# The last group of a two-layer decoder: its tail beside the shared expert, the router's choice inside the expert blocks, inner rows of the final feed-forward in the wait for a gather, and bulk loads issued earlier

## What is computed

```python
for e in range(E):
    m = topi == e
    sel = m.any(axis=-1)
    wmean = (topw * m).sum() / jnp.maximum(m.sum(), 1)
    y = _mlp(xf, expert_gate_w[e], expert_up_w[e], expert_down_w[e])
    out = out + jnp.where(sel[:, None], y * wmean, 0)
out = out + _mlp(x, shared_gate_w, shared_up_w, shared_down_w)
```

## Time and profile before

| | us |
|---|---|
| median of 3 runs | 2366.88 (2365.27 to 2369.79) |
| profiled execution | 2361.88 |
| its span, first to last instruction | 2360.1 |
| PE / DVE / ACT / POOL busy | 1914.0 / 1671.1 / 1110.2 / 846.1 |
| mean granted TensorE clock | 0.908 of full speed |

### The profile page before, as it was taken

The page is one execution under the profiler, slowest core; times in us unless marked ns, Lnnn a source line. Parts: engine busy times, 40 slices in busy tenths (PEclk is TensorE's granted clock), DMA queues, the critical chain, the costliest instruction groups (busy, mean ns, idle before and its releaser), DMA issues.

```text
span 2360.1 us, 39753 instructions
## 1 busy us (share of the span) xinstructions
PE 1914.0 (81%) x14136; PEld 1359.2 (58%) x14136; DVE 1671.1 (71%) x4073; ACT 1110.2 (47%) x3152; POOL 846.1 (36%) x775
## 2 busy tenths in 40 slices
PE   2786688878897898788898789789887889775698
PEld 1455356745685467645685457645774568563355
DVE  8895795679947794769756994789567975713355
ACT  3463266435653466436642566246543565332243
POOL 0552363316512462327421661336332652111000
PEclk7997799979997999889997999799988999787799
DMA  3000010402040012201040103001130204070000
GB/s 133 11 1 10 12 61 6 128 10 72 1 122 12 24 58 60 74 19 63 6 126 12 38 36 116 18 23 59 30 104 10 72 1 129 5 256 19 10 14 23
DMA packets 72748, 117.09 MB, mean 50 GB/s; under 512 B 7823, under 2 KB 46871, under 8 KB 72039
## 3 DMA queue, kind: packets, MB, share of 16 engines
q1 hardware_dynamic: 67014, 101.42, 13.3%
q0 software_dynamic: 5536, 13.12, 1.9%
HBM read 95.18 MB, written 18.81 MB: 48 GB/s over the span
## 4 chain that ended last, share of the span: by engine, by line
DVE 38%; PE 35%; issue 12%; POOL 6%; ACT 6%; DMA 3%; SPq 1%; DVEq 0%; POOLq 0%; ACTq 0%
PE bank L1392 32%; DVE work L513 11%; DVE bank L522 5%; DVE work L531 3%; DVE work L511 3%; ACT work L984 3%; POOL hid L1298 2%; DVE max L821 2%; PE bank L1396 2%; POOL work L1278 1%; ACT act_row L984 1%; DMA y_sorted<-y_quad 1%; POOL work L1273 1%; DVE acc L733 1%; DMA w_ring<-in_w_routed 1%
## 5 line engine op out<-in xcount | busy, mean ns | idle before, releaser
L1392 PEld LDWEIGHTS bank<-work 128*128 128x128 f32 (+2 forms) x5152 | 388.4, 200 | 164.2 <-issue 160.6
L1392 PE MATMUL bank<-work 128*128 128x128 f32 (+2 forms) x5152 | 419.6, 308 | 50.2 <-DMA work<-in_wo 25.4
L984 ACT ACTIVATE work<-bank 128x512 f32<-128x512 f32 (+1 forms) x560 | 246.9, 519 | 275.9 <-PE bank L1392 244.7
L513 DVE TENSOR_TENSOR work<-bank,table_space 64x512 f32<-64x512 f32 x512 | 352.2, 688 | 6.8
L1266 POOL TENSOR_TENSOR work<-work 128x512 f32<-128x512 f32 x128 | 163.4, 1277 | 332.7 <-DVE work L513 231.3
L984 ACT ACTIVATE work<-work 128x512 f32<-128x512 f32 (+1 forms) x338 | 196.6, 618 | 140.6 <-DVE work L601 81.4
L984 ACT ACTIVATE work<-work,negmax 128x128 f32<-128x128 f32 x512 | 199.2, 390 | 100.2 <-DVE negmax L533 100.2
L1273 POOL TENSOR_TENSOR work<-sb_ident,nrm 128x512 f32<-128x512 f32 x128 | 133.2, 1041 | 275.0 <-ACT nrm L984 275.0
L1392 PE MATMUL bank<-work,table_space 128*128 128x512 f32 x256 | 140.4, 630 | 89.9 <-DVE negmax L533 59.4
L984 ACT ACTIVATE hid<-bank,w_ring 128x128 f32<-128x128 f32 x480 | 136.4, 370 | 138.3 <-PE bank L1392 138.2
L511 DVE TENSOR_TENSOR work<-bank,table_space 128x512 f32<-128x512 f32 x256 | 173.8, 679 | 30.2 <-POOL work L1278 18.3
(11 more groups left out here) (293 smaller groups left out, 3327.2 us busy)
## 6 DMA issues: line engine op xcount, KB each, us to landing
w_ring<-in_w_routed SPq DMA_DIRECT2D x120, 514.0 KB, 4.8
x_quad<-x_sorted SPq DMA_DIRECT2D x24, 256.0 KB, 2.9
y_sorted<-y_quad SPq DMA_DIRECT2D x24, 256.0 KB, 4.4
x_T<-in_x_T POOLq DMA_DIRECT2D x9, 256.0 KB, 3.0
x_row<-in_x_row POOLq DMA_DIRECT2D x9, 256.0 KB, 4.1
ctx_T<-in_ctx_T SPq DMA_DIRECT2D x8, 256.0 KB, 2.7
work<-in_ctx_row SPq DMA_DIRECT2D x8, 256.0 KB, 3.1
out<-act_row SPq DMA_DIRECT2D x8, 256.0 KB, 2.3
```

Source lines behind the costliest of these rows:

```text
L513: last = v.tensor_tensor(rows(wk[i + 1][o]), rows(src[p]), sinT[o, s].unsqueeze(1).broadcast_to([DH0, GB, N]), ALU.mult)
L984: return nc.scalar.activation(o, i, f, **k)
L1392: return nc.tensor.matmul(o, l, r, start=start, stop=stop, skip_group_check=True)
```

## The change

Six edits, all in the last group and phase 2.

1. **Tail beside the shared expert.** `last_experts` replaces `heads_and_experts(G - 1, ...)` on PE, ACT and DVE. On PE the tail of group 6 is interleaved with the shared expert; on DVE its two layernorms use `inverse_root`; POOL issues four of the eight scatters before its part of the tail.
2. **SP order.** The bulk loads go ahead of `first_blocks(G - 1)`, for groups 0 to 5; group 6's and 7's activations are copied from SBUF by `keep_tail`; the five first weight loads go ahead of the wait for the scatter.
3. **Choice in two halves.** `choose` runs in five steps, for groups 0 to 6 between the blocks of the last group, for group 7 where the whole choice was.
4. **Seven `block_up`s early.** All five of group 0 and two of group 1 are issued right behind the last block, and PE, DVE and ACT do them before `experts_norm`. Their results lie in the weight ring.
5. **`experts_norm`** takes its root from DVE.
6. **Phase 2** starts with what is left of group 1, before the means are known; the down products of groups 0 and 1 follow in two runs. The choice is transposed straight from `sel1`, without a copy on POOL.

```diff
@@ SP
+            def keep_tail(g):
+                sp.wait_ge(t_T_sb, g * LNS + LNS)
+                sp.dma_start(x5T_all[:, g], seq_T[:]).then_inc(stored, 16)
+                sp.dma_start(x5_all[:, g], act_row[0][:].rearrange("p b d -> p (b d)")).then_inc(stored, 16)
             def first_blocks(g):
+                if g == G - 1:
+                    sp.wait_ge(owners_in, g + 1)
+                    for j in range(RING):
+                        load_weights(j)
                 sp.wait_ge(scattered, g * (TOPK * GB * 16) + TOPK * GB * 16)
...
             g = G - 1
-            store_tail(g, -1)
-            first_blocks(g)
             sp.wait_ge(attn_out, G)
             for name in phase2:
                 sp.dma_start(late[name], a[name]).then_inc(in2, 16)
-            sp.wait_ge(stored, 32 * g + 16)
-            sp.dma_start(x5T_all[:, 0:g], ...); sp.dma_start(x5_all[:, 0:g], ...)
+            sp.wait_ge(stored, 32 * (g - 1) + 16)
+            sp.dma_start(x5T_all[:, 0:g - 1], ...); sp.dma_start(x5_all[:, 0:g - 1], ...)
+            first_blocks(g)
+            keep_tail(g - 1)
             blocks(g)
-            sp.wait_ge(t_T_sb, g * LNS + LNS)
...
+            keep_tail(g)
@@ DVE
+            def choose(step, lo, k):
+                n = k * GB
...
+                if step == 0:
+                    dve.wait_ge(rl_a, 2 if lo else 1)
+                    link(v.tensor_scalar(ex, ex, 1.0, None, ALU.add))
+                    link(v.reciprocal(pr, ex))
+                if step == 1:
+                    best(pr, oh1, m1)               # five instructions
+                    link(v.scalar_tensor_tensor(t, oh1, -4.0, pr, ALU.mult, ALU.add))
+                if step == 2:
+                    best(t, oh2, m2)
...
+            def last_experts(g):
+                for i in (1, 2):
+                    if i == 1:
+                        tail_out(g, -1)
+                    else:
+                        tail_mix(g, -1)
+                    dve.wait_ge(norm_t.stats, tally(g, -1, LNS, i + 1))
+                    inverse_root(norm_t)
+                    centre_of(norm_t, g, i, -1)
+                tail_logits(g, -1)
+                take_rows(0, g)
+                add_shared(g)
+                for i in range(BLOCKS):
+                    take_block(i, g)
+                    if i in (1, 5, 9):
+                        take_rows(i // GB + 1, g)
+                    if i in (3, 5, 7, 9, 11):
+                        choose((i - 3) // 2, 0, G - 1)
+                dve.wait_ge(in2, in2_all)
+                v.tensor_copy(sel2b[:], late["sel2"]).then_inc(sel_cast, 1)
+                for p in range(BLK):
+                    hidden1(p, 0)
+                for p in range(AHEAD):               # AHEAD = 2
+                    hidden1(p, 1)
@@ ACT
+            def last_experts(g):
+                norm_tail(g, 1, bank[2], act_row[1], -1, True)
+                gelus(0, g)
+                t_to_T(g, 1, bank[7], -1)
+                norm_tail(g, 2, bank[6], act_row[0], -1, True)
+                gelus(1, g)
+                t_to_T(g, 2, bank[2], -1)
+                router_exps(0, G - 1)
+                for j in range(2, UNITS):
+                    gelus(j, g)
+                choices1(0)
+                for p in range(PAIRS):
+                    silu1(p, 0)
...
@@ POOL
-            tail(G - 1, -1)
             pool.wait_ge(slots_in, G)
-            for i in range(TOPK * GB):
+            for i in range(GB):
                 scatter(G - 1, i)
+            tail(G - 1, -1)
+            for i in range(GB, TOPK * GB):
+                scatter(G - 1, i)
@@ PE
+            def last_experts(g):
+                tail_out(g, -1)
...
+                experts_up(0, g, 0, False)
+                tail_mix(g, -1)
+                experts_up(1, g, 0, False)
+                tail_T(g, -1)
+                experts_down(0, g, 0, False)
+                tail_logits(g, -1)
+                experts_down(1, g, 0, False)
+                rows_T(0, g, 0, False)
+                experts_up(2, g, 0, False)
+                for j in range(3, UNITS + 1):
...
+                pe.wait_ge(in2, in2_all)
+                choices_of(0)
+                for p in range(BLK):
+                    if p == PAIRS:
+                        choices_of(1)
+                    block_up(p, 0)
+                for p in range(AHEAD):
+                    block_up(p, 1)
+            last_experts(G - 1)
+            pe.wait_ge(h_done, BLK + AHEAD)
             project2(G - 1, False)
             attn1(G - 1, G, False)
...
+            for p in range(AHEAD, PAIRS):
+                block_up(p, 1)
+            choices_of(2)
+            pe.wait_ge(sums_done, 2)
...
+            block_up(PAIRS, 1)
+            pe.wait_ge(norm_f.out, 1)
...
+            block_up(0, 2)
+            for p in range(BLK):
+                block_down(p, 0)
+            block_up(1, 2)
+            for p in range(BLK):
+                block_down(p, 1)
```

More of the change, by code:

```diff
@@ L286, in first_blocks @@
                 load_rows(1)
-                for j in range(RING):
-                    load_weights(j)
+                if g < G - 1:
+                    for j in range(RING):
+                        load_weights(j)
             def blocks(g):
@@ L1848, in _, with choices_of @@
                 attn1(g, g + 2, True)
-            heads_and_experts(G - 1, 1, False, True, True)
+            def choices_of(k):
+                pe.wait_ge(sums_done, 1 if k < G - 1 else 2)
+                if k == 0:
+                    pe.wait_ge(y_out, G * BLOCKS)
+                else:
+                    pe.wait_ge(selT_sb, k)
+                for b in range(GB):
+                    last = nc.tensor.transpose(bank[6][0:8, b * N:b * N + N], sel1[:, k, b], ident[:])
+                last.then_inc(selT_ps, 1)
@@ new lines, in block_down @@
+            def block_down(p, g):
+                pe.wait_ge(h_done, g * BLK + p + 1)
+                if p == 0 and g == 0:
+                    pe.wait_ge(scaled, 1)
+                elif p == 0:
+                    pe.wait_ge(sum_read, g)
+                for b in range(GB):
+                    last = mm(rows(bank[7])[:, b], rows(hidden_tile(g, p))[:, b], late["w_d1"][:, p],
+                              start=p == 0 and b == 0, stop=p == BLK - 1)
+                if p == BLK - 1:
+                    last.then_inc(y4, 1)
@@ L1855, in _ @@
             tail_logits(G - 1, 0)
-            pe.wait_ge(sums_done, 1)
-            mm(bank[0][0:8, 0:1], router_sum[:, 0], ones_col)
-            mm(bank[0][0:8, 1:2], router_sum[:, 1], ones_col, start=False).then_inc(tot, 1)
-            pe.wait_ge(in2, in2_all)
+            for p in range(AHEAD, PAIRS):
+                block_up(p, 1)
+            choices_of(2)
+            pe.wait_ge(sums_done, 2)
+            for i in range(2):
+                for half in range(2):
+                    last = mm(bank[7][0:8, i:i + 1], router_sum[:, half, i], ones_col, start=i + half == 0)
@@ L1886, in block_down @@
-            def block_down(p, g, d):
-                pe.wait_ge(h_done, tally(g, d, BLK, p + 2))
-                if p == 0:
-                    pe.wait_ge(sum_read, tally(g, d, 1, 1))
-                for b in range(GB):
-                    last = mm(rows(bank[7])[:, b], rows(wk[2 + p])[:, b], late["w_d1"][:, p],
-                              start=p == 0 and b == 0, stop=p == BLK - 1)
-                if p == BLK - 1:
-                    last.then_inc(y4, 1)
-            def ffn1(g, d, before):
-                block_up(0, g, d)
-                if before:
-                    block_down(BLK - 1, g, d - 1)
-                for p in range(1, BLK):
-                    if p == PAIRS:
-                        transpose_choices(tally(g, d, 1, 2))
-                    block_up(p, g, d)
-                    block_down(p - 1, g, d)
@@ L1908, in _ @@
[L1908 to L1912 removed]
+            block_up(0, 2)
[4 more added lines that the diff above has]
+                block_down(p, 1)
+            block_up(2, 2)
+            block_down(0, 2)
+            block_down(1, 2)
+            block_up(3, 2)
+            block_down(2, 2)
@@ L1915, in layouts @@
+            choices_of(3)
+            block_up(4, 2)
+            block_down(3, 2)
+            for g in range(3, G):
+                block_up(0, g)
+                block_down(BLK - 1, g - 1)
+                for p in range(1, BLK):
+                    if p == PAIRS and g + 1 < G:
+                        choices_of(g + 1)
+                    block_up(p, g)
+                    block_down(p - 1, g)
+            block_down(BLK - 1, G - 1)
 def layouts(inp):
```

271 lines of the change are left out of this document (155 added, 116 removed).

## The result

| | before | changed |
|---|---|---|
| median, us | 2368.03 (2365.27 to 2369.79, 4 runs) | 2325.49 (2323.84 to 2328.05, 4 runs) |
| ratio to before | | 0.9823, 95% interval 0.9808 to 0.9837 |
| profiled execution / its span | 2361.88 / 2360.1 | 2324.63 / 2322.8 |
| PE / DVE / ACT / POOL busy | 1914.0 / 1671.1 / 1110.2 / 846.1 | 1902.5 / 1679.9 / 1111.7 / 844.3 |
| mean granted clock | 0.908 | 0.918 |

Faster, 2331 predicted and 2325.5 measured. To see where the 37.3 us between the two spans went, I cut both traces at the same events: the output product of group 6's second attention (2061.92 in the earlier trace rows, 2059.43 now), the first block's up product, the end of the last down product, `combine`, the normalised rows, the last logits on DVE, the last `acc` addition, the end.

What follows compares the result with a forecast made beforehand. Bounds: a weight-load wait in group 7's blocks, then its gather, then PE alone in phase 2. -9.8 + 4.3 - 30.7 = -36.2 us, from the median 2366.88 to 2331; own range 2325 to 2337, 80% range 2323 to 2342.

Steps and rivals of the forecast that it cites:

- A: Bulk loads issued at 1994 meet group 6's gather: +0.3 us, bounds 0 and 8.
- Rival 5: Group 6's gather is late by the bulk loads, 8 us: 2339 us, chance 0.05.
- B: Group 6's tail beside the shared expert, output product to first block: +0.9 us, bounds -4 and +5.
- C: Expert blocks of group 7, to the last down product: weight waits go, blocks 1.79 us apart; -11.0 us for the stretch.
- rival 1: In group 7's blocks the weight ring decides again, 3 to 4 us more: 2335 us, chance 0.12.
- Rival 2: DVE's `choose` steps become the bound between the blocks, 10 us onto the path: 2340 us, chance 0.07.
- D: Group 7's gather wait: early products start `combine` 2.8 us later, the root on DVE adds 1.6 less 0.1; +4.3 us.
- Rival 3: The early products outrun the gather at the lower clock, 7 x 2 us more: 2345 us, chance 0.07.
- rival 4: DVE's multiplications hold group 7's eight gather issues, 5.4 us in all, 2.7 past the fill: 2334 us, chance 0.03.
- E: Phase 2: shorter start 3.7, old lower-clock restart 2.8, products done earlier or within the start 24.2; -30.7 us.
- rival 6: Slower than before: PE isn't granted the full clock in phase 2, about 2430 us, chance 0.02.

Runs made afterwards that it cites:

- before_again: The kernel before, unchanged, run once more for its trace: 2361.21 us, ratio 0.9999.
- bulk_late: Changed kernel with phase 2's bulk loads issued behind `first_blocks` again, first weights still early: 2323.51 us, ratio 0.9831.
- after_again: The changed kernel, unchanged, run once more beside the kernel before: 2324.05 us, ratio 0.9827.
- bulk_alone: Kernel before with only the bulk loads moved behind group 6's last store, and groups 6 and 7 copied from SBUF: 2352.16 us, ratio 0.9958.
- old_tail: Changed kernel with group 6's tail ahead of the shared expert again on PE, ACT and DVE, roots on ACT: 2326.7 us, ratio 0.9865.
- no_ahead: Changed kernel with only group 0's five up products in the gather's wait, group 1's two back behind the logits: 2325.41 us, ratio 0.9843.
- copy_first: Changed kernel with ACT making each transposed copy before the pair of gelus in group 6's tail: 2324.65 us, ratio 0.9838.
- act_root: Changed kernel with the root of the last `experts_norm` on ACT again: 2324.0 us, ratio 0.9844.
- no_fill: Changed kernel with the seven early `block_up`s moved behind the logits, to the start of phase 2: 2337.75 us, ratio 0.9892.

## Why the prediction was right

**A (+0.3): right.** The bulk took the DMA engines to 0.99, and group 6's `combine` started 2.55 us after its last gather issue, before 2.62. Over all traces it started 2.50 to 2.62 after that issue in the three whose bulk goes out later (before, before_again, bulk_late; mean 2.57) and 2.49 to 3.52 in the eleven others (mean 2.84), so the term is 0.27 on average and 1.0 at most. Rival 5 is out. The gather's last issue came as the bulk drained (DMA share 0.91 in the microsecond ahead of it, 0.37 behind), as the forecast had it. All of the bulk had been issued by 1992.23, just ahead of the gather's first issue at 1992.32, and yet the gather's packets did not all wait for it: of 256, 129 were moved by 2003.3, while the bulk ran, but the first came over 4 us after the first issue, where the kernel before had 19 in the second microsecond. The rule of the Trainium skill ("DMA: Bandwidth & Descriptors", Queues, rings and completion order), that a DMA engine takes the rows that have work in turn, agrees with the two queues moving side by side; strict order of arrival does not. What the forecast did not see is that the place at 1994 isn't needed: the bulk has only to be through before the first refill (bulk_late).

**B (+0.9): the sign is right, the size isn't settled.** It is +2.0 between the first two traces and +0.3 between before_again and after_again. The four traces with the old order (before, before_again, bulk_alone, old_tail) have 25.88 to 27.67, nine with the new one 27.80 to 27.90, and the tenth, no_ahead, 32.19 in the same code. What of its terms can be looked up was right: PE waits 2.10 for the copy behind the gelus, the table loads at 2079.68 and 2084.89 are off the path. But such terms can't simply be added here, because a product's length depends on the level of the clock that it meets (copy_first); the forecast's bounds allowed for that, its sum did not.

**C (-11.0 for the stretch): right, with two parts off that cancel.** The wait of 7.84 is gone and the blocks are 1.79 apart. The last down product ended at 2117.84 where 2119.5 was forecast, but this trace came to the last part 2.5 us earlier. Between blocks 0 and 1 stood 1.79 us of shared down product (2088.69 to 2090.48 before), not 1.2. Against that, the later waits for weights did not go: with an idle of 0.17 ahead of it the one before block 13 was 0.86 in all, and the changed kernel had 0.34 and 1.41, so these waits are 0.9 longer where -0.9 and +1.0 were forecast. The +1.0 was to be DVE or ring; it was the ring. In the eleven other traces in which nothing stands ahead of the refills that wait is 0.53 to 0.74, as it was in the kernel before, and C is 29.06 to 29.72 (31.50 in bulk_alone, where the shared down product still stands between the blocks). So rival 1, at 3 to 4 us more, didn't happen. Rival 2 didn't either: with `choose` behind the blocks C was no shorter.

**D (+4.3): the mechanism was right, two sizes were low.** Measured +5.6. `combine` waits for `hidden1` and not for the gather, as said. Five of the fill's six `block_up`s with a choice took 2.23 and not 2.13, and PE stopped 0.85 for a bank that DVE had yet to read, which the sum did not have; together 1.35, of which the fill's earlier start gave back 0.2. The root on DVE cost 1.61 for 1.5 (act_root gives it back). Rival 3 didn't happen: full clock over the whole fill. Nor rival 4: the gather issues beside DVE's multiplications took 0.95 to 0.98 us, before 0.960 on average, and the rows were there when DVE came to them. The Trainium skill's rule ("SBUF — State Buffer", SBUF: two separate sides) is about DVE instructions in a two-port mode or with two inputs in SBUF. Each of these float32 multiplications has one of its inputs in a bank of PSUM, so the rule doesn't name them, and the rival had less behind it than it seemed; this trace agrees.

**E (-30.7): right, -31.8 measured.** The first product came directly behind the last logits (2202.57, DVE has them at 2202.76), and the first down product at 2214.89, 12.1 after them where 12.5 was forecast; from there to the last addition it was 101.3, forecast 102.0. PE was busy 92.89 of 93 us from 2222 at a clock of 1.00, so rival 6 is out. bulk_alone and no_fill split the term: the choice off the path and the new order 13.9, the products in the fill 17.4.

**The sum.** Forecast -36.2; the traces give -37.3 over the span, -34.8 in the part that the change touches. The errors of the terms are +1.1, +1.3 and -1.1, and 0.3 each in A's term and in the attention stretch. The absolute number was 5.5 high, and the measured 2325.49 lies at the lower edge of the forecast's own range, 2325 to 2337. The forecast of the difference stood on a trace, the number on the first median of before, 2366.88: in later sets of runs the same kernel had 2361.1 to 2364.0, against 2324 to 2325.5 for the changed one. By these medians the change is worth 36 to 40 us. That five terms came out with errors of no more than 1.4 us is partly luck, since equal code differs by 2 us and more from trace to trace.

By edits, from traces of one run each, so good to 2 us: bulk loads -10.3 to -13.0, choice between the blocks (with the new order of phase 2) -11 to -14, early `block_up`s -13.2, tail beside the shared expert 0, root on DVE in `experts_norm` +1.6.

## What to carry to other kernels

Where one engine is saturated at the end of a kernel, count what can be pulled out of that stretch in that engine's own time, and fill its idle time elsewhere: a filler that outlasts the wait was neither gain nor loss to within 1.4 us (no_ahead), and one that stays inside it counted nearly in full: against no_fill, the five products of group 0 in no_ahead took 12.1 us off phase 2 and cost 0.4 ahead of `combine`. A load that nobody is waiting for yet should not be in front of a ring refill; that alone was over a quarter of the gain, and one of two ways to get it would have done. Shortening a wait among short products may buy nothing when they then run at the lower clock, so look at the durations behind the wait before counting it.

## What the runs showed of the hardware that was not expected

- Throwaway products that end 1.48 us before the next real one didn't save the projections behind them from the lower clock (1.92 for 1.02); the same products with no stop before the transposes did. One trace each.
- Equal code took unequal time: the same tail took 27.9 and 32.19 us, attention 2 with its tail 59.88 to 62.52, a group of phase 1 254.98 to 260.64. The longer ones have more of their products at the lower clock where this was looked up; that it is the clock everywhere is not shown. Single executions of the kernel before spread from 2354 to 2372, some 0.4% either side, so single edits under 5 us were read from stretches and not from medians.
- Eight indirect DMA issues took 0.95 to 1.03 us each (mean 988 ns, before 982) beside a bulk stream that filled the DMA engines, and 0.95 to 0.98 in another stretch beside DVE at half load. Beside the bulk their packets went out in between its own: 64 of them with 671 of the bulk's in 4 us.
